# Second attention of a four-block kernel: the order of value products, key/value projection and output drain

## The reference, cut to what matters

```
x = x + _L1_xattn_ref(_layernorm(x), ctx_4096, mask, Wq, Wk, Wv, Wo, q_norm_w, k_norm_w)

q = (hidden @ Wq.T)  -> 32 heads of 128        k, v = (ctx @ Wk.T), (ctx @ Wv.T) -> 8 heads of 128
q, k = rmsnorm(q), rmsnorm(k)                  each key/value head serves 4 query heads
probs = softmax(q k^T / sqrt(128) + mask)      within each sequence of 64 rows
out   = (probs @ v) @ Wo.T
```

## Time and profile before

| | us |
|---|---|
| median of 3 runs (lowest, highest) | 1523.95 (1519.75, 1524.34) |
| the profiled execution | 1523.5 |
| its span, first to last instruction | 1521.7 |
| start of step 0, start of step 31 | 523.9, 1452.2 |
| a step with c = 0, 1 or 3 and without stalls, such as the one at 1038.4 | 29.17 |
| a step with c = 2 and without stalls (four more matmuls for the next weights' scale) | 29.6 |

### The profile page before, as it was taken

How to read it: one execution, slowest core, us unless ns; L and a number is a source line. 1 busy time by engine, 2 the same in 40 slices (tenths; PEclk the granted TensorE clock), 3 DMA queues, 4 the chain that set the end, 5 groups by cost and what they waited for, 6 DMA issues and landing times.

```text
span 1521.7 us, 27579 instructions
## 1 busy us (share of the span) xinstructions
PE 1464.0 (96%) x9895; PEld 845.7 (56%) x9895; DVE 1123.7 (74%) x2172; ACT 795.4 (52%) x3201; POOL 711.1 (47%) x668
## 2 busy tenths in 40 slices
PE   5999999999999788999999999999999999999998
PEld 4888645555554445555555555555555555555554
DVE  5888777778877668766776677677677677667868
ACT  5678731212123565545654754664565465555763
POOL 5678875554565353334333333434333343334553
PEclk9999999999999899999999999999999999999999
DMA  7444345442434464643453455345445445434622
GB/s 246 160 159 141 122 85 116 110 72 40 77 76 77 115 136 73 132 93 66 95 90 80 86 82 98 77 81 105 80 73 104 85 71 99 72 56 67 100 51 111
DMA packets 358936, 146.87 MB, mean 97 GB/s; under 512 B 342304, under 2 KB 342688, under 8 KB 356112
## 3 DMA queue, kind: packets, MB, share of 16 engines
q1 hardware_dynamic: 357504, 137.77, 44.7%
q10 hardware_dynamic: 1296, 7.34, 1.4%
HBM read 58.02 MB, written 4.19 MB: 41 GB/s over the span
## 4 chain that ended last, share of the span: by engine, by line
PE 51%; DVE 6%; ACT 4%; POOL 2%; DMA 2%; SPq 1%; issue 1%; DVEq 0%; POOLq 0%; ACTq 0%
PE bank L72 16%; PE bank L74 16%; PE bank L73 16%; PE bank L2430 3%; ACT a_prob L1829 2%; DMA a_pT_lo<-a_p_lo 1%; POOL a_prob L1704 1%; DVE a_oT_lo L2098 1%; POOL a_xr_lo L1726 1%; ACT a_oT_lo L1806 1%; SPq L1609 1%; SPq L1619 1%; DMA a_kT_lo<-a_kn_lo 1%; DVE x_res L2185 1%; DVE x_res L2023 0%
## 5 line engine op out<-in xcount | busy, mean ns | idle before, releaser
L1829 ACT ACTIVATE a_prob<-a_prob,a_nmx 128x64 f32<-128x64 f32 x512 | 170.2, 334 | 180.0 <-DVE a_nmx L2074 180.0
L72 PE MATMUL bank<-w,a_oT_hi 128*128 128x512 f16 x512 | 193.9, 379 | 2.8 <-DVE a_oT_lo L2098 2.0
L74 PE MATMUL bank<-w,a_oT_hi 128*128 128x512 f16 x512 | 194.0, 379 | 0.0
L73 PE MATMUL bank<-w,a_oT_lo 128*128 128x512 f16 x512 | 194.0, 379 | 0.0
L72 PE MATMUL bank<-w,xT_hi 128*128 128x448 f16 (+1 forms) x512 | 188.2, 368 | 2.1 <-DVE h L1231 2.0
L73 PE MATMUL bank<-w,xT_lo 128*128 128x448 f16 (+1 forms) x512 | 187.8, 367 | 0.0
L74 PE MATMUL bank<-w,xT_hi 128*128 128x448 f16 (+1 forms) x512 | 187.8, 367 | 0.0
L1704 POOL TENSOR_TENSOR a_prob<-a_prob,a_mask 128x512 f32<-128x512 f32 x64 | 79.9, 1270 | 199.8 <-DVE a_prob L2068 199.8
L2023 DVE SCALAR_TENSOR_TENSOR x_res<-bank,a_oinv,x_res 128x512 f32<-128x512 f32 x128 | 95.5, 746 | 72.5 <-PE bank L74 72.5
L1157 ACT CAST f_h_hi<-h 128x448 f16<-128x448 f32 x64 | 35.6, 563 | 209.6 <-DVE h L1231 209.5
L1716 POOL TENSOR_TENSOR a_krs<-a_kve,neg_half 128x4 f32<-128x4 f32 x32 | 32.8, 1024 | 239.5 <-DVE a_kve L2048 239.5
(11 more groups left out here) (351 smaller groups left out, 4120.4 us busy)
## 6 DMA issues: line engine op xcount, KB each, us to landing
shared<-in_l_wq SPq DMA_DIRECT2D x8, 1024.0 KB, 5.0
shared<-in_l_wo SPq DMA_DIRECT2D x8, 1024.0 KB, 5.1
shared<-in_w ACTq DMA_DIRECT2D x8, 896.0 KB, 4.6
craw<-in_w SPq DMA_DIRECT2D x11, 512.0 KB, 3.8
a_wide<-in_l_ctxT SPq DMA_DIRECT2D x16, 256.0 KB, 3.9
x_res<-in_x SPq DMA_DIRECT2D x16, 256.0 KB, 4.6
shared<-in_ctx SPq DMA_DIRECT2D x16, 256.0 KB, 4.4
shared<-in_l_wkv SPq DMA_DIRECT2D x8, 512.0 KB, 3.8
```

The costliest lines, as they stand in the source:

```text
L72: pe.matmul(out, a_hi, b_hi, start=first, stop=False)
L73: pe.matmul(out, a_lo, b_hi, start=False, stop=False)
L74: return pe.matmul(out, a_hi, b_lo, start=False, stop=last)
L1829: ins = act.activation(pt, pt, ACT.Exp, bias=nmx[:, col:col + 1], accum_out=den[:, col:col + 1])
```

## The change

It has three parts. PE: A1 is issued straight behind A0, and K3 behind A1. ACT: `keys_values(i+1, 0)` is taken ahead of `outputs(i, 0)`, and `outputs(i, 1)` ahead of `keys_values(i+1, 1)`. DVE: `values(i+1, 0)` ahead of `output_hi(i)`, and `outputs(i, 1)` ahead of `values(i+1, 1)`, `key_squares` and `query_sums`. No instruction, wait or buffer is added or removed.

```diff
@@ ACT, body
                 query(i + 1, 2)
                 query(i + 1, 3)
+                keys_values(i + 1, 0, (c + 1) % 2)
                 outputs(i, 0, range(1, 2))
-                keys_values(i + 1, 0, (c + 1) % 2)
+                outputs(i, 1)
                 keys_values(i + 1, 1, (c + 1) % 2)
-                outputs(i, 1)
                 keys(i + 1)
@@ DVE, body
                 query(i + 1, 3)
+                values(i + 1, 0, (c + 1) % 2)
                 output_hi(i)
...
                 outputs(i, 0)
                 if ahead and c == 3:
                     query_eps2(g + 1)
-                values(i + 1, 0, (c + 1) % 2)
+                outputs(i, 1)
                 values(i + 1, 1, (c + 1) % 2)
...
                 key_squares((c + 1) % NCH, i + 1)
                 query_sums(i + 1)
-                outputs(i, 1)
                 add_out(c, i, 0)
@@ PE, body
                 attend(i, 0, c % 2)
-                keys_values(cn, i + 1, range(3, TPC))
                 if fresh and c == 0:
                     pe.wait_ge(s_cs, 6)
                 attend(i, 1, c % 2)
+                keys_values(cn, i + 1, range(3, TPC))
                 out_rows(i, 0, o_weights)
```

## The result

The changed kernel takes 1527.5 us (median of 8 runs, 1525.5 to 1530.2), the kernel before in the same series 1522.6 (8 runs, 1519.8 to 1524.7). The ratio is 1.0035, with an interval of 1.0024 to 1.0046: slower by about a third of a per cent, 5 us. A second series gave 1.0026 (1.0017 to 1.0036). The profiled executions are 1527.05 and 1523.5, a difference of 3.55 us; 1.6 was forecast. So the time lies inside the range given for 8 in 10 (1520.5 to 1529.5), but the loss is two to three times the one that was added up.

The account below looks back on a forecast made before the run. PE was taken to bound the kernel, busy 96% of the span. PE's row 0, late transposes +2.2, earlier keys -0.6, step 0 0: +1.6 on 1523.5 gives 1525.1 us; 8-in-10 range 1520.5 to 1529.5.

Parts of the forecast that it names:

- PE's row and the copy: Second attention: O waits for DVE's copy, stays 3.03 after A0; PE's shorter row becomes 0.29 idle; value 0.
- The drain rival: O follows PE's row: two fewer form changes save 0.19 in all steps, 1517.6, with all of the 0.29 1514.5; chance 0.06.
- Bank 0 ahead of the outputs: ACT and DVE: 1.33 us of work fits in 1.35 before output_hi, copy not late; cost 0, bounds 0 and 0.7.
- The ACT rival: Bank 0's work makes outputs(i, 0) and output_hi late in more than the tight steps: 1528.2; chance 0.07.
- The keys 0.3 earlier: DVE makes keys 0 to 0.42 earlier, 0.3 taken; counts at steps 11 and 30: -0.6, bounds 0 and -0.8.
- Step 0: A1 waits for L1974, PE idle some 1 us at clock 0.50, A1 and K3 done before O; cost 0.
- The clock rival: PE's idle time in step 0 keeps the clock low another 3.4 us, costing 1.7: 1526.8; chance 0.04.
- A1's wait: A1, 0.66 behind A0, waits for the second transpose in eight steps: seven at 0.14, step 25 at 1.17; +2.2.
- The transpose rival: Second transpose lands over 0.9 us after A0's start in most steps, not eight: up to 1534.4, middle 1530; chance 0.10.

Follow-up runs that it names:

- the kernel whose copy is 1.76 late: PE's and DVE's parts of the change on the kernel before, ACT keeping its old order: 1581.2 us, ratio 1.0385.
- the high parts first: O's tile 0 takes its eight high-part products first, four low-part last: ratio 0.9991 on the kernel before; 1522.9 us, 1.0013 on the changed order.
- The mixtures: High-part products first; old order with c = 0 and step 30, changed order elsewhere: 1518.8 us, 0.9984; old order also in seven more steps: 1517.5, 0.9976.

## Why the prediction came out as it did

**PE's row and the copy: right.** O is at 3.03 in every undisturbed step, 0.146 to 0.147 behind the copy's end, and two changes of form fewer became 0.29 of idle time. The forecast that the waits would name L2098 was wrong: K3's last matmul is shown until 703.06 + 0.27 = 703.33, 0.13 before O, and no wait is listed for so short a gap, before and after. The drain rival falls, by the changed kernel itself and by the kernel whose copy is 1.76 late. Its 0.20 per step shows in O's place, but only with the high parts first.

**Bank 0 ahead of the outputs: right.** `output_hi` is at 0.87 in all steps from 1 to 30, with c = 0 too, so 1.33 of work did fit in 1.35. Even in step 12, where I had allowed 0.08, it isn't late. The ACT rival falls.

**The keys 0.3 earlier: right.** L2053 went from 6.79 to 6.49 behind A0, K of step 30 waits 0.31 less, the weight load of step 11's scores no longer waits for `a_kT_lo`. Outside A0 to O the steps are 0.47 shorter in sum, where -0.6 was put. The size rests on both parts together, which I had not seen.

**Step 0: put at nothing, and not settled.** The first profile shows no loss there, but by luck. Windows of step 0, before, after, and in the second profile of the changed kernel; the last line is the stretch behind A0 of that second profile (columns as above):

```profile
523.89:558.88 34.99, 30.75 (x206) 17.42 (x207) 20.47 (x55) 17.45 (x84) 14.56 (x13) 0.87 0.51 90
```

```profile
525.02:558.83 33.81, 29.36 (x205) 17.23 (x206) 20.64 (x55) 17.53 (x84) 14.65 (x13) 0.91 0.53 94
```

```profile
526.06:562.68 36.62, 32.16 (x206) 18.05 (x206) 20.66 (x55) 17.55 (x84) 14.71 (x13) 0.83 0.49 88
545.70:552.50 6.80, 5.78 (x37) 3.41 (x38) 4.65 (x14) 1.83 (x4) 0.00 (x0) 0.50 0.83 126
```

In the first profile the step starts 1.13 later and is 1.18 shorter. The shorter time comes ahead of A0: the clock is at 0.50 until 527.66, for 2.64 us of the step, instead of until 529.33, for 5.4, which no part of the change touches. Behind A0 the clock is low from 544.7 to 548.1, as long as the 543.0 to 546.4 of the earlier trace rows. In the second profile the step is 1.63 longer than before. PE is idle for 0.99 between A0 and A1, waiting for L1974 as forecast; the clock stays at 0.50 (1.2 GHz) from 545.7 to 552.5, and A1 to the last of K3 takes 6.17 - 2.45 = 3.7 us at it, not 2.5. O follows K3 there, at 6.38 behind A0, while the copy ends at 5.08. The clock rival had 1.7 for this, at a chance of 0.04. PE's part alone, PE's and ACT's, and the changed order without the second transpose do the same: low for 6.8 us, step 0 at 36.4 to 36.5. Where K3 stands between A0 and A1 and the clock was low for as long ahead of it (the kernel before and ACT's and DVE's part alone), it is low for 3.4 and the step takes 34.9 to 35.0. That the idle time keeps the clock low is argued from this; no run moved it alone, and the old order without the second transpose is low for 6.8 too, though from 540.5 on, ahead of its A0, and with step 0 at 34.2. How often it happens in the timed runs isn't known: over the second series the granted clock is 0.992 on average in both kernels.

**A1's wait: right in kind, too small.** Forecast +2.2, measured +4.07; this is the term of the sum that was mis-sized. By steps (us beyond 3.03, after): 12 0.21, 14 0.57, 16 0.12, 17 0.41, 20 0.99, 23 0.17, 24 0.13, 25 1.01, 28 0.33 (0.08 of it there before), 30 0.22. For six of the eight steps that I named it came as worked out: 12, 16, 24, 28 and 30 have 0.12 to 0.25 where I had 0.14 (1.0 was meant for seven of them), and 25 has 1.01 where I had 1.17. Step 21 has none, by 0.04 of margin. What the sum lacks is step 20, with 0.99 instead of 0.14, and 14, 17 and 23, which I had as early enough: 0.99 + 0.57 + 0.41 + 0.17 = 2.14, of which 2.0 were not in the forecast.

Why these four? I had taken the landings from the trace before and let them stand. They didn't. The tile `a_pT_lo` in step 20, first in the kernel before, then after:

```profile
L1629 SPq DMA_TRANSPOSE a_pT_lo<-a_p_lo x2: 1188/1226/1264, 1139.4 to 1140.7; - x2
DMA to landing us min/median/max: 2.5/2.5/2.5
```

```profile
L1629 SPq DMA_TRANSPOSE a_pT_lo<-a_p_lo x2: 1188/1231/1274, 1140.5 to 1141.7; - x2
DMA to landing us min/median/max: 2.4/2.9/3.4
```

The second one takes 3.4 instead of 2.5. DMA traffic of the kernel after between its issue and its landing, 1141.7 to 1145.1 (packets, MB, share of the 16 engines):

```profile
q1 hardware_dynamic: 1516, 0.37, 61.3%
q14 instruction: 1, 0.01, 0.7%
```

The same stretch with PE's part alone, 1145.6 to 1148.3, where it took 2.5:

```profile
q1 hardware_dynamic: 1104, 0.27, 51.1%
```

A packet of instructions falls among the transpose's own. In the kernel before there is one too, but in the stretch 1144.2 to 1145.2, when the transpose had landed (1143.16). I followed this through the traces: in steps 17, 20 and 23 the longer of the two transposes takes 3.2 to 3.5 in the changed kernel, again in its second profile, with ACT's and DVE's part alone and with PE's and ACT's, each time with a packet of queue 14 some 1.5 to 2.3 behind the issue; in the kernels that keep ACT's list (PE's part alone, PE's and DVE's, before with the high parts first) it takes 2.5 in all three steps. In step 14 both are long (2.8 to 3.4) with the new list, and only one (3.0 to 3.2) with the old one, with O at 3.03 where PE's part is alone. The mixtures, which switch all three lists step by step, agree. So the late landings of these four steps come with ACT's list, not with PE's or DVE's. That the packet is ACT's instructions, and that it is what delays the transpose rather than a sign of it, is inferred from this coincidence; no run moved the packet alone. For it speaks that the same holds where no list was touched: in steps 5 and 8 the first low transpose takes 3.0 to 3.2 in all 13 profiles, with a packet of queue 14 some 1.7 to 1.9 behind the issue. Against a simple rule: the second one of these steps has the same packet 0.5 to 0.6 behind its issue and takes 2.5. Why one packet costs 0.7 to 0.9 us stays open.

The transpose rival (landings late in most steps, 1530) was partly true: its mechanism made the rest of the loss, in three steps more than forecast and for longer in a fourth, not in most. I had written against it that nothing in the change delays SP, DVE's low probabilities or POOL. As far as the issues go that held; the error was to take from it that the landings stay where they were. The medians differ by 4.3 to 4.9 us, steps 1 to 30 of the two profiles by 3.60 and 4.16; whether the rest is step 0 or scatter isn't settled.

## What to carry to other kernels

An order that puts two consumers of late data side by side saves something only if the engine's own row sets the end; read first what the next stage starts on (here a copy, 0.146 us before it in every step), and remove that, or the saving becomes idle time. A wait that was hidden by the work between is to be priced with the scatter of what it waits for, not with its value in one trace: here the landings moved when another engine's list was reordered. Parts of a reordering on three engines are one edit: here one alone cost 8 us and the other 5, against 4 for both. And a stretch that looks untouched in one pair of profiles can hide two differences that cancel, as step 0 did; compare a second profile before calling it so.

## What the hardware showed that I had not expected

- SBUF transposes of 128x512 in 16 bits land 2.5 us after their issue, but 3.0 to 3.5 where an 8 KB instruction packet (queue 14) falls 1.5 to 2.3 us behind it, and 3.6 to 4.5 in step 25 of the eleven profiles that have the second one, where a 16 KB packet (queue 8) falls 1.0 to 1.9 behind it (4.1 before, 4.0 after). Traffic of the kernel after in step 25, 1287.5 to 1291.9:

```profile
q1 hardware_dynamic: 1288, 0.31, 53.2%
q8 instruction: 1, 0.02, 1.7%
```

- Reordering 3 of ACT's calls, with the same instructions, went with such packets falling 2.4 to 2.6 us earlier, after against before, relative to the transposes in four steps of 31, the same steps in each kernel that has the list.
- Where DVE's copy sets O, PE starts 0.146 to 0.147 us behind its end, whether the trace lists a wait or not; and leaving or entering the 64-row form costs 0.10 each time.
- TensorE's granted clock behind A0 of step 0 was at 0.50 for 3.4 us in the kernel before and for 6.8 in four profiles with A1 behind A0, where PE had been idle for 1 us before A1; step 0 was some 1.6 us longer there.
